# Two chosen experts of eight: lists of rows made on chip and gathered per block, in place of rows scattered to their places

## The reference

```
xn = layernorm(x)                                  # per token, 128 features
log_alpha = (xn @ router_w.T + router_b) / max(temperature, 0.1)
for _ in range(3):                                 # 8 experts, 512 tokens of a sequence
    log_alpha -= logsumexp(log_alpha, over experts)
    log_alpha -= logsumexp(log_alpha, over tokens)
gates = exp(log_alpha); gates /= gates.sum(over experts) + 1e-8
two largest gates per token, scaled to the sum 1
y = sum over the two chosen experts e of gate_e * (relu(xn @ wg[e]) * (xn @ wp[e])) @ wo[e]
x = x + xn + y
```

## Time and profile before

| | us |
|---|---|
| median of three runs | 6526.69 |
| lowest and highest | 6521.57, 6538.94 |
| profiled execution, its own time | 6507.51 |
| its span, first to last instruction | 6505.7 |

### The profile page before, as it was taken

How to read it: one execution, slowest core, us unless ns; L and a number is a source line. 1 busy time by engine, 2 the same in 40 slices (tenths; PEclk the granted TensorE clock), 3 DMA queues, 4 the chain that set the end, 5 groups by cost and what they waited for, 6 DMA issues and landing times. The chain is left out here.

```text
span 6505.7 us, 95125 instructions
## 1 busy us (share of the span) xinstructions
PE 4965.4 (76%) x29755; PEld 2574.5 (40%) x30008; DVE 3701.5 (57%) x7740; ACT 3366.0 (52%) x5243; POOL 1256.0 (19%) x1147
## 2 busy tenths in 40 slices
PE   5999718748888842948777846689999999999466
PEld 1333318724444432932222234433333334343444
DVE  4333344467767763556666666167666666756561
ACT  4888515425555531627666702266666666666122
POOL 1000033333334305321111006500000000000056
PEclk9999858869999966979999957799999999999577
DMA  3333511213333341132222122300000000000214
GB/s 79 73 76 79 81 37 51 69 40 89 88 85 90 90 60 43 50 82 60 59 63 65 49 61 41 71 1 0 0 0 0 0 0 0 0 0 0 61 33 91
DMA packets 297981, 311.38 MB, mean 48 GB/s; under 512 B 60950, under 2 KB 248566, under 8 KB 297604
## 3 DMA queue, kind: packets, MB, share of 16 engines
q1 hardware_dynamic: 265180, 269.54, 17.0%
q0 software_dynamic: 32448, 37.39, 2.9%
HBM read 193.60 MB, written 112.80 MB: 47 GB/s over the span
## 5 line engine op out<-in xcount | busy, mean ns | idle before, releaser
L953 ACT ACTIVATE prob_relative<-slot_relative 128x1024 f32<-128x1024 f32 x512 | 500.0, 1042 | 146.9 <-PE obank_relative L827 140.5
L3300 ACT ACTIVATE prob_wide<-slot_wide 128x1024 f32<-128x1024 f32 x512 | 493.8, 1016 | 149.7 <-PE slot_wide L3199 149.7
L1271 DVE TENSOR_TENSOR slot_decay<-slot_decay,dtab_decay 128x512 f32<-128x512 f32 (+3 forms) x1024 | 453.9, 493 | 168.1 <-PE slot_decay L787 148.4
L953 ACT ACTIVATE prob_rms<-slot_rms 128x1024 f32<-128x1024 f32 x512 | 498.0, 1040 | 85.3 <-PE slot_rms L802 83.4
L953 ACT ACTIVATE prob_decay<-slot_decay 128x640 f32<-128x640 f32 x512 | 358.6, 705 | 344.7 <-PE slot_decay L808 344.0
L3199 PE MATMUL slot_wide<-qT_wide,kT_wide 64*128 64x512 f32 x2048 | 508.8, 615 | 2.9 <-ACT prob_wide L3300 2.9
L2675 POOL DMA_INDIRECT xg_choice_b<-xn_rows_choice_b,ids_choice_b x64 | 85.4, 1334 | 2072.6 <-DVE ids_choice_b L2951 2053.4
L1283 DVE TENSOR_TENSOR prob_relative<-prob_relative,rtab_relative 128x512 f32<-128x512 f32 (+1 forms) x512 | 409.8, 849 | 128.3 <-ACT prob_relative L953 119.0
L3212 PE MATMUL obank_wide<-prob_wide,v_wide 128*64 128x512 f32 x2048 | 467.7, 598 | 1.8 <-DVE zT_wide L3357 1.8
L827 PE MATMUL obank_relative<-prob_relative,vaug_relative 128*32 128x512 f32 x2048 | 291.7, 644 | 116.6 <-DVE prob_relative L1283 115.0
L3343 DVE TENSOR_TENSOR sums_wide<-sums_wide,prob_wide 128x1024 f32<-128x1024 f32 x256 | 313.6, 1225 | 28.7 <-ACT prob_wide L3300 0.2
(11 more groups left out here) (748 smaller groups left out, 10320.7 us busy)
## 6 DMA issues: line engine op xcount, KB each, us to landing
scratch_decay<-parts_decay SPq DMA_DIRECT2D x192, 128.0 KB, 2.4
qst_rms<-scratch_rms SPq DMA_DIRECT2D x64, 288.0 KB
kst_rms<-scratch_rms SPq DMA_DIRECT2D x192, 96.0 KB
qst_relative<-scratch_relative SPq DMA_DIRECT2D x64, 288.0 KB
kst_relative<-scratch_relative SPq DMA_DIRECT2D x192, 96.0 KB
qst_decay<-scratch_decay SPq DMA_DIRECT2D x128, 128.0 KB
scratch_rms<-parts_rms SPq DMA_DIRECT2D x96, 128.0 KB, 2.3
kst_decay<-scratch_decay SPq DMA_DIRECT2D x192, 64.0 KB
```

The lines of the kernel that those rows point to most:

```text
L953: nc.scalar.activation(prob[:, Q % 2, j, 0:c1 - c0], slot[:, u % 3, c0:c1], ACT.Exp).then_inc(exp_done, 1)
L1271: last = nc.vector.tensor_tensor(sl, sl, dtab[:, h, 0:m], ALU.mult)
L3300: nc.scalar.activation(prob[:, Q % 2, u % 4, :], slot[:, u % 2, :], ACT.Exp).then_inc(exp_done, 1)
```

## The change

- **Scores from raw X.** TensorE transposes X itself and multiplies it by the router's weights. Since the layer norm is a shift and a scale per token, VectorE corrects the scores afterwards with the mean, the reciprocal deviation and the column sums of the weights (`shift`, `colsum`), for all 64 tiles at once. The statistics are computed in one group of 64 tiles. The scores of all sequences share one PSUM bank. The temperature is folded into the scale.
- **Normalising elsewhere.** The rows `xn` are normalised by GpSimd (8 sequences, two operations each) and by ScalarE (8 sequences, 32 instructions, inside its last five steps of the scoring).
- **One table set.** ScalarE loads the set that has Exp and Ln at the stage's start.
- **No scatter into place.** SP stores `xn` with its gates as it is (`xn_rows`, four DMAs) once the gates are there. The blank rows, the targets and the token columns go.
- **Lists by one-hot products.** VectorE splits each token's row number into lane and block. In four groups of 16 tiles it makes a one-hot matrix of the lanes (128x2048, one comparison) and 16 of the blocks, scaled by the token's number plus one (128x91 each). TensorE adds the 64 products in one PSUM bank. The sum holds, for each block and lane, the number of the token there, or zero. VectorE makes the lists of sources (`from_row`) and targets (`to_row`) of it.
- **Gathers.** GpSimd gathers the rows of each block into the ring by an indirect DMA, 12 ahead, and then one after each scatter. SP's fetches go.
- **Additions to X** of the normalised rows: 16 pieces of 128x512 inside the blocks 12 to 27, in place of four of 128x2048 ahead of the loop.
- The experts of the blocks are computed with one block per partition and turned by a matmul. Two kinds of semaphores now last over both stages (`lasting`, with `turn` as the number of the stage).

The diff, cut to its core:

```diff
@@ SP @@
-                sp.wait_ge(blank_ready, 1)
-                sp.dma_start(by_block[:, :, 0:TOKEN], blank[:].unsqueeze(1).to_broadcast([P, BLOCKS, TOKEN])
-                             ).then_inc(blanked, 16)
-                sp.dma_start(by_block[:, :, TOKEN:C], dump[:].bitcast(F32)).then_inc(blanked, 16)
...
-                sp.wait_ge(rows_placed, 16 * T)
-                for k in range(BLOCKS):
-                    if k >= RING:
-                        sp.wait_ge(y_sent[k % RING], 16 * (k // RING))
-                    sp.dma_start(xg[:, k % RING, :], xg_rows[k * P:(k + 1) * P, :]).then_inc(fetched[k % RING], 16)
+                sp.wait_ge(xn_by_act, NB - BY_POOL)
+                sp.wait_ge(xn_by_pool, BY_POOL)
+                sp.wait_ge(gates_ready, 1)
+                for g in range(NB // GROUP):
+                    at = slice(g * GROUP * TPB, (g + 1) * GROUP * TPB)
+                    sp.dma_start(out_rows[:, at], xn[:, at]).then_inc(xn_stored, 16)
+                sp.wait_ge(x_added, 1)
@@ TensorE @@
                 for b in range(NB):
-                    pe.wait_ge(xn_ready, b + 1)
                     if b >= 2:
                         pe.wait_ge(xT_ready, b - 1)
                     for t in range(TPB):
-                        last = nc.tensor.transpose(bench[:, b % 2, t * P:(t + 1) * P], xn[:, b * TPB + t, 0:D], ident[:])
+                        last = nc.tensor.transpose(bench[:, b % 2, t * P:(t + 1) * P], X[:, b * TPB + t, :], ident[:])
...
+                for i in range(T):
+                    g, j = i // LIST, i % LIST
+                    if j == 0:
+                        pe.wait_ge(onehots, g + 1)
+                    last = nc.tensor.matmul(bench[:, 0, 0:BLOCKS], lane1h[:, g % 2, j, :], block1h[:, g % 2, j, :],
+                                            start=(i == 0), stop=(i == T - 1), skip_group_check=True)
@@ ScalarE @@
+                nc.scalar.preload_act_table_set("natural_log_exp_and_others")
...
+                        last = nc.scalar.activation(xn[:, i, 0:D], X[:, i, :], ACT.Identity, bias=stats[:, i, 10:11],
+                                                    scale=stats[:, i, 9:10])
...
+                    if b >= NB - LAST_FIVE:
+                        for _ in range(2 if b < NB - 2 else 1):
+                            normalise_x(by_act.pop(0))
@@ GpSimd @@
-                for i in range(T):
-                    nc.gpsimd.indirect_dma_start(
-                        xg_rows, bass.IndirectOffsetOnAxis(ap=spots[:, at:at + 1], axis=0), xn[:, i, :],
-                        None).then_inc(rows_placed, 16)
+                def gather(k):
+                    nc.gpsimd.indirect_dma_start(
+                        xg[:, k % RING, :], None, xn_rows,
+                        bass.IndirectOffsetOnAxis(ap=from_row[:, k:k + 1], axis=0)).then_inc(fetched[k % RING], 16)
+                pool.wait_ge(rows_listed, 1)
+                pool.wait_ge(xn_stored, 16 * (NB // GROUP))
+                for k in range(RING):
+                    gather(k)
+                pool.wait_ge(targets, 1)
+                for k in range(BLOCKS):
+                    scatter(k)
+                    if k + RING < BLOCKS:
+                        gather(k + RING)
@@ VectorE @@
+                for g in range(T // LIST):
+                    at = slice(g * LIST, (g + 1) * LIST)
+                    if g >= 2:
+                        dve.wait_ge(listed, g - 1)
+                    nc.vector.tensor_tensor(lane1h[:, g % 2], parts[:, 0, at].unsqueeze(2).to_broadcast([P, LIST, P]),
+                                            count[:].unsqueeze(1).to_broadcast([P, LIST, P]), ALU.is_equal)
+                    for j in range(LIST):
+                        i = g * LIST + j
+                        last = nc.vector.tensor_scalar(block1h[:, g % 2, j, :], count[:, 0:BLOCKS], parts[:, 1, i:i + 1],
+                                                       number_of[:, i:i + 1], ALU.is_equal, ALU.mult)
+                    last.then_inc(onehots, 1)
...
                     hidden(k)
                     both_parts(k - 1)
+                    if RING <= k < RING + NB:
+                        last = add_normalised(k - RING)
```

More of the change, by code:

```diff
@@ L125, in fresh, with lasting @@
         return self.ctx.enter_context(self.nc.semaphore(name))
+    def lasting(self, name):
+        if name not in self.last:
+            self.last[name] = self.fresh(name)
+        return self.last[name]
     def next_stage(self):
@@ L2043, in pair_feed_forward @@
     GROUP = 4
+    LAST_FIVE = 5
     ctx = ExitStack()
@@ L2117, in pair_feed_forward @@
         y_filled, part_ready, yg_ready, x_added = sem("y_filled"), sem("part_ready"), sem("yg_ready"), sem("x_added")
+        rounds = [(BLOCKS - 1 - u) // RING + 1 for u in range(RING)]
         y_back = [sem(f"y_back{g}") for g in range(NB // GROUP)]
@@ L2270, in _, with normalise_x @@
             def _(act):
+                nc.scalar.preload_act_table_set("natural_log_exp_and_others")
+                def normalise_x(b):
+                    act.wait_ge(stats_ready, 1)
+                    for i in range(b * TPB, (b + 1) * TPB):
+                        last = nc.scalar.activation(xn[:, i, 0:D], X[:, i, :], ACT.Identity, bias=stats[:, i, 10:11],
+                                                    scale=stats[:, i, 9:10])
+                    last.then_inc(xn_by_act, 1)
+                by_act = list(range(BY_POOL, NB))
                 for b in range(NB):
@@ L2376, in take_scores @@
-                def take_scores(b):
-                    dve.wait_ge(sc_filled, b + 1)
-                    nc.vector.tensor_tensor(gate[:, :, b, :], ybank[:, b % 2, 0:TPB * E].rearrange("p (t e) -> p t e", e=E),
-                                            rb[:].unsqueeze(1).to_broadcast([P, TPB, E]), ALU.add).then_inc(sc_drained, 1)
-                gather_statistics(0)
-                for b in range(NB):
-                    normalise_x(b)
-                    if b >= 2:
-                        take_scores(b - 2)
-                    if b % GROUP == 1 and b // GROUP + 1 < NB // GROUP:
-                        gather_statistics(b // GROUP + 1)
@@ L2487, in _ @@
-                link(nc.vector.reduce_sum(ownkey[:], owner[:], AX_X))
-                link(nc.vector.tensor_copy(ownint[:], ownkey[:]))
-                link(nc.vector.tensor_scalar(experts[:, :, 0], ownint[:], 4, None, ALU.arith_shift_right))
-                nc.vector.tensor_scalar(experts[:, :, 1], ownint[:], 15, None, ALU.bitwise_and).then_inc(experts_ready, 1)
-                for g in range(NB // GROUP):
-                    at = slice(g * GROUP * TPB, (g + 1) * GROUP * TPB)
-                    last = nc.vector.tensor_tensor(X[:, at], X[:, at], xn[:, at, 0:D], ALU.add)
```

192 lines of the change are left out of this document (118 added, 74 removed).

## The result

| | kernel before | changed kernel | ratio |
|---|---|---|---|
| the measurement the forecast was for | 6542.74 us (nine of ten 6521.57 to 6562.06, one 7518.19) | 6473.95 us (6458.69 to 6512.24) | 0.9898, 0.9878 to 0.9919 |
| the same two kernels in a later job | 6507.42 us | 6347.93 us | 0.975, 0.9734 to 0.9766 |
| profiled execution: own time, span | 6507.51, 6505.7 us | 6484.57, 6482.8 us | |

The forecast was 6332 us, a gain of 195. The measurement gave 69. The second line of the table is the same change, unaltered, 160 us faster than the kernel before. Both levels came back in later jobs (a job is one sitting on one chip, with all its kernels run in it); what separates them is told in the experiments.

The account below looks back on a forecast made before the run. Stages had different bounds: in a pair stage, VectorE's statistics held TensorE, 64 scatters filled placing, TensorE set the loop. 26.4 + 5.4 + 0.5 + 65.3 = 97.6 us a stage, 195 in both, from 6526.7 to 6332; range 6295 to 6400.

Parts of the forecast that it names:

- Loop: Expert block loop: TensorE still sets 2.79 us a block, GpSimd needs 2.5, so no cost apart from the rivals.
- Rival (c): Block loop: VectorE's work delays GpSimd's descriptors, GpSimd becomes the bound; 46 us a stage, 6424 us; chance 0.15.
- Scoring: Scoring part: TensorE transposes raw X without waiting for VectorE, iterations start at 810.0, not 836.46; 26.4 us a stage.
- Rival (b): Scoring part: the scores run at 2.4 GHz; 17 us more gained a stage, 6298 us; chance 0.07.
- Tables: Softmax iterations: one table set removes ScalarE's loads between Exp and Ln; 5.4 us a stage.
- fields: Pair stage: a 128x64 step and a memset of the token columns go; 0.5 us a stage.
- Placing: Row numbers to first expert matmul: lists and gathers replace 64 scatters, 33.6 us against 98.9; 65.3 us a stage.
- Rival (a): Placing part: the list's matmuls stay at 1.2 GHz and TensorE bounds; 4 us lost a stage, 6341 us; chance 0.2.
- Additions to X, gathers in the loop: Block loop: additions of 0.6 us fit VectorE's 1.3 idle, gathers fit GpSimd's time; no cost.
- Outside the change: Unaltered stages: the sum had no term for them.

Follow-up runs that it names:

- f0: The changed kernel itself, no edit, run again in a later job without late signals: 6347.93 us, 0.975 of the kernel before.
- h1: Changed kernel with SyncE's plain transfers bringing the rows and one spare GpSimd gather per block into a tile nobody reads: 6475.48 us.
- i3: Changed kernel with rows of 528 bytes and 74 idle TensorE products in the first pair stage, moving the decay loop's code: 6459.11 us.
- i1: Changed kernel with rows of 528 bytes and 10 idle TensorE products in the first pair stage, moving the decay loop's code: 6447.96 us.
- h3: Changed kernel with each gather replaced by a plain transfer of 66 KB from the same GpSimd queue, choice of rows left out: 6355.21 us.

## Why the prediction was right or wrong

Against the measurement it was wrong, in the step **Loop**: "Bounds of the loop: 0 to the rivals below", and among them was none in which GpSimd keeps its pace and TensorE's signals come late. In the first job each loop cost 53 us (311.2 from the first expert matmul to the last scatter, against 258.2 in f0). Rival (c) named 46 us a stage for another reason, a slow GpSimd, which the gathers' 977 ns rule out. In jobs without late signals the step is right to 0.4 us: 257.8 before, 258.2 after, and TensorE never waits for a gather in the loop. It was closer than forecast: GpSimd took 2.6 us a block in the first stage and 2.7 in the second, of 2.79, and not 2.5.

There was a sign. The profile I worked from had its own time 19 us under the median of the runs. I took that as a constant and added it. It was the difference between two kinds of job: 6507.5 is what the kernel before takes in jobs without late signals, 6526 to 6543 in the others.

The 126 us between the forecast gain and the measured one are, to within 1 us: 106.7 in the two loops, 23.8 in unaltered stages that f0 shows as well, 12.6 by which the altered parts were sized too high, and 19.3 elsewhere in the first job, less the 35.3 us by which the kernel before was slower there too. That the two kinds of job exist could be seen in the 19 us; that gathers are what pays in one of them, no row of the prediction could tell.

Against run f0 the steps can be checked one by one (158.8 us between the two spans, of 195):

- **Scoring**: 26.4 forecast, 26.7 measured. Rival (b) fell: the clock stayed at 0.50.
- **Tables** 5.4 and **fields** 0.5: 5.7 measured together. There are no loads between Exp and Ln.
- **Placing**: 65.3 forecast, 59.2 measured. The step took TensorE to be warm from the second group on. Rival (a) was the truth, its chance of 0.2 too low: a pass took 0.216 us at a clock of 0.50, not 0.112, and TensorE, not VectorE, set the pace. The clock rose only in the loop, some 5 us after its first product.
- **Additions to X, gathers in the loop**: nothing, as forecast. By the Trainium skill (SBUF — State Buffer, SBUF: two separate sides) VectorE's fp32 copy of 0.43 us a block should hold up GpSimd's descriptors. The prediction took the 0.97 us of the earlier trace rows for a trace that doesn't agree, but there the copy began 0.12 us after the scatter. Where GpSimd's DMA begins during the copy, the trace of f0 agrees: in its second loop 13 gathers that did took 1.18 us, and 62 apart from a copy 0.98. It costs nothing here because 2.7 us are still under 2.79. One of the 13:

```profile
2500.55 0.43 DVE L2583 COPY pair_up_top_b<-up_top_b 128x512 f32 x1 [0.40 <-issue]
2500.63 1.19 POOL L2388 DMA_INDIRECT xg_top_b<-xn_rows_top_b,from_row_top_b  x1 [0.30 <-issue]
```

- **Outside the change**: 0 forecast. The decay stage took 19.8 us more, and the other stages together 4.0.

26.7 + 5.7 + 59.2 less 0.9 at the loop and the end make the first stage's 90.7; the second gained 91.8. With 19.8 and 4.0 off, that is 158.8.

## What to carry to other kernels

Run the control first: the unaltered change beside its variants, in the same job. Four variants without it looked like four successful cures of something that wasn't there. And when a profile's own time differs from the median of the runs by more than their spread, find out why before forecasting from it.

Where many gathers are interleaved with TensorE's work, count on a price of some 0.6 us per gather (53 us over 91) in part of the jobs, five of seven here; plain transfers and scatters didn't have it. And after any change in the number of TensorE's instructions, look at the unaltered loops behind it: a pause "issue" at the loop's turn that wasn't there before is code that arrives late, and a few idle instructions ahead can cure it (10 here; 74 cost 13 us at another place).

## What the runs showed of the hardware

A gather by GpSimd can hold up TensorE's signals: the product is shown as run, and ScalarE waits up to 2.3 us for its signal in the loop of h1, 7.5 at the start of the first job's loop. At the start of the loop in the first job, while the first twelve gathers ran back to back:

```profile
914.65 1.91 PE L2268 MATMUL pbank_top_a<-xt_top_a,pair_up_top_a 128*128 128x128 f32 x8
...
916.60 0.60 ACT L2343 ACTIVATE relu_top_a<-gbank_top_a 128x512 f32<-128x512 f32 x1 [3.15 <-issue]
...
918.09 1.06 PE L2268 MATMUL pbank_top_a<-xt_top_a,pair_up_top_a 128*128 128x128 f32 x8
...
922.60 0.95 POOL L2388 DMA_INDIRECT xg_top_a<-xn_rows_top_a,from_row_top_a  x1 [0.30 <-issue]
925.47 0.60 ACT L2343 ACTIVATE relu_top_a<-gbank_top_a 128x512 f32<-128x512 f32 x1 [7.46 <-remote]
```

The first `relu` follows its product at once, with gathers running, and that product still took 1.91 us, the 1.2 GHz level. The second product took 1.06, the 2.4 GHz level, ended at 919.15, and its `relu` starts at 925.47, 2.87 us after the last of the twelve gathers was issued (in f0 a gather lands 2.7 us after its issue). Four signals with 25 passes between them were recorded within 0.3 us, at 925.45 to 925.74: they had piled up.

The hold-up goes with the higher clock. In i3 the granted clock rose to the 2.4 GHz level at 909.0, during the 74 idle products and before the first rows were transposed; ScalarE's copy waits for the first two transposes:

```profile
912.98 0.41 PE L2257 MATMUL bench_top_a<-ident_top_a,xg_top_a 128*128 128x128 f32 x2
925.69 0.43 ACT L2341 COPY xt_top_a<-bench_top_a 128x128 f32<-128x128 f32 x2 [36.67 <-remote]
```

In i1, of the same job, the first of them ran at the 1.2 GHz level beside the same gathers:

```profile
911.28 0.45 PE L2257 MATMUL bench_top_a<-ident_top_a,xg_top_a 128*128 128x128 f32 x1 [2.34 <-DMA xg_top_a<-xn_rows_top_a,from_row_top_a]
911.77 0.27 ACT L2341 COPY xt_top_a<-bench_top_a 128x128 f32<-128x128 f32 x1 [22.77 <-PE bench_top_a L2257]
```

So a signal was 12 us late in i3 and on time in i1. The pair stages of the ten profiles with late signals say the same: of the signals whose product ended within 1.2 us after a gather's start, all 49 at the 1.2 GHz level came within 0.02 us, and 176 of 204 at the 2.4 GHz level over 0.1 us late. No run was made to vary the clock alone.

It isn't only the signals. In the second pair stage of the first job, TensorE's own passes come singly while the last gathers run (issued at 2450.76, 2452.01 and 2453.27); in f0 these eight passes have no such gaps:

```profile
2450.80 0.72 PE L2268 MATMUL pbank_top_b<-xt_top_b,pair_up_top_b 128*128 128x128 f32 x5
2452.00 0.27 PE L2268 MATMUL pbank_top_b<-xt_top_b,pair_up_top_b 128*128 128x128 f32 x1 [0.48 <-issue]
2453.39 0.27 PE L2268 MATMUL pbank_top_b<-xt_top_b,pair_up_top_b 128*128 128x128 f32 x1 [1.12 <-issue]
```

What holds them up stays open. The jobs with late signals differ in one more thing that the traces show: they keep fewer landing marks. Of the 1456 marks of the 91 gathers of the first pair stage (16 each), the first job's trace holds 842 and f0's 1454. h3 holds 648 of its plain transfers' 1456, with no late signal there, so the missing marks go with the kind of job and not with the hold-up. Whether recording the trace has a part in the hold-up was not tested.
